# Second cross attention: the mask multiply moves from GpSimd to VectorE, both evacuations of turned probabilities to ScalarE

## The chip, the cores and the metric

The kernel runs on one core of one Trainium2 chip. The metric is the device time of one execution in microseconds (us), the median of several runs. One execution was also taken by the hardware profiler, which gives the rows below. The engines are called TensorE (PE in rows; PEld is its weight load), VectorE (DVE), ScalarE (ACT), GpSimd (POOL) and SyncE (SP, which here issues all the DMAs).

## The reference, cut to what matters

The whole program is a two-layer latent transformer: a cross attention, a linear attention and a mixture block, then a second cross attention, a multi-query attention and a second mixture. Only the second cross attention is touched. It attends from 256 query rows to 4096 key rows with 16 heads of dimension 16 and relative positions:

```python
content = einsum('bthd,bThd->bhtT', q + r_w_bias, k)
rel = einsum('bthd,bThd->bhtT', q + r_r_bias, pe)
rel = _relative_shift(rel)      # pad one column, reshape, drop one row
attn = (content + rel) * (1.0 / sqrt(HEAD_DIM))
attn = attn * mask - 1e10 * (1.0 - mask)
p = softmax(attn, axis=-1)
out = einsum('bhtT,bThd->bthd', p, v)
```

Everything is float32; the products of queries and keys are made from bfloat16 parts.

## The kernel before, in words

The function `cross1` has three blocks, and the second holds the loop. A unit of work is one head, one tile of 128 query rows and one half of the keys, so a unit is a score tile of 128x2048 and there are 16 x 2 x 2 = 64 units. Each unit is handled in two parts of 1024 columns (`SUB`). The scale is already in the queries. The tile `row` has four buffers, one for each of the four units of a head (`U = 4`).

What happens to unit c, in the order of its data:

- TensorE makes the relative scores in `rel_ps` (L1732, one PSUM tile of 128x1024), ScalarE copies them to `out0` or `out1` (L1816), and SyncE stores them to DRAM (L1683) with a row pitch of 4097, and reads them back shifted into `row` (L1672). This is done four units ahead.
- TensorE makes the content scores in `cont_ps` (L1732, also one PSUM tile of 128x1024). VectorE adds them to `row` (L1872, `add`), once for each part.
- GpSimd multiplies `row` by the mask (L1851), once for each part.
- VectorE adds `minus`, which is 1e10 * (mask - 1), and takes the maximum (L1881, `top_of`), once for each part; then small instructions make the negated maximum (L1887) and keep it (L1890).
- ScalarE takes the exponential of the whole 128x2048 tile (L1821).
- TensorE transposes the probabilities in `turn_ps` (L1750, `turn`, one PSUM tile for both parts in turn). ScalarE evacuates part 0 (L1827) and VectorE part 1 (L1897) into `turned`.
- TensorE weighs the values (L1763, `weigh`) into `sum_ps`. VectorE copies `sum_ps` to `sumsT` (L1903, `sums_out`). TensorE brings the four partial sums together in `both` (L1773, `bring_together`), and VectorE keeps the result (L1908, `keep_sums`).

All engines run the same loop of slots. In slot c each engine does, in its own written order, what its list says for units c (scores), c-1 (exponential), c-2 (turn and weigh), c-3 (sums) and c+4 (relative scores). There is no planner: the order on an engine is the program's order, and semaphores tie the engines together. TensorE's order in a slot, which the change does not touch, is: content(c, 0); bring_together(c-3), which waits for `sums_sb`, that is for VectorE's `sums_out` of unit c-3; turn(c-2, 0); relative(c+4, 0); content(c, 1), which waits until VectorE's add of part 0 has emptied `cont_ps`; turn(c-2, 1); weigh(c-2, 0); relative(c+4, 1); weigh(c-2, 1).

VectorE's order in a slot before is: top_of(c-1, 0); sums_out(c-3); add(c, 0); top_of(c-1, 1); add(c, 1); copy_turned(c-2); keep_sums(c-3).

Of the kernel before, what the change touches and what calls it, by code (L numbers as in the profile page):

```python
# [17 lines left out]
ALU = mybir.AluOpType  # L18
# [11 lines left out]
HALF = S2 // NHALF  # L30
# [1476 lines left out]
SUB = HALF // 2  # L1507
CPS = SUB // P
UNITS = H * U
# [3 lines left out]
def cross1(f, mask):  # L1513
# [8 lines left out]
    with ExitStack() as ctx:  # L1522
# [90 lines left out]
        with ExitStack() as inner:  # L1613
# [23 lines left out]
            def where(p, c):  # L1637

                return 2 * U * p + c, 2 * p + c // U, c % U, c // U % 2, c % U // NHALF, c % NHALF

            def slots(eng, slot, before=None):

                for n in range(-U, 3):
                    slot(0, n, n)
                with eng.Fori(0, LOOPS) as p:
                    for c in range(3, 3 + 2 * U):
                        slot(p, c, None)
                for n in range(2 * U * LOOPS + 3, UNITS + 3):
                    slot(LOOPS, n - 2 * U * LOOPS, n)

            def runs(n, ahead):

                return n is None or 0 <= n + ahead < UNITS
# [148 lines left out]
            @block.scalar  # L1802
            def _(act):
                act.sem_inc(s["rel_out"], 1)

                def evacuate(p, c, part):
                    n, head, u, b, t, half = where(p, c)
                    act.wait_ge(s["rel_mm"], 2 * n + part + 1)
                    if part == 0 and u >= NHALF:
                        act.wait_ge(rel_stored[u - NHALF], 16 * (head + 1))  # L1810
                    elif part == 0 and not (isinstance(n, int) and n < U):
                        act.wait_ge(rel_stored[u + NHALF], 16 * head)
                    elif part == 0 and u == 0:
                        act.wait_ge(s["zero_set"], 1)
                    out = out1 if half else out0[:, 1:HALF + 1]
                    nc.scalar.copy(out[:, part * SUB:(part + 1) * SUB], rel_ps[:]).then_inc(s["rel_out"], 1)  # L1816

                def exponentials(p, c):
                    n, head, u, b, t, half = where(p, c)
                    act.wait_ge(s["top_ready"], n + 1)  # L1820
                    nc.scalar.activation(row[:, u], row[:, u], ACT.Exp, bias=ntop[:, u:u + 1]).then_inc(s["exp_done"], 1)  # L1821

                def copy_turned(p, c):
                    n, head, u, b, t, half = where(p, c)
                    act.wait_ge(s["turned"], 2 * n + 1)
                    act.wait_ge(s["weighed"], 2 * n + 1)
                    nc.scalar.copy(turned[:, 0].rearrange("p k n -> p (k n)"), turn_ps[:]).then_inc(turned_sb[0], 1)  # L1827

                def slot(p, c, n):
                    if runs(n, -2):  # L1830
                        copy_turned(p, c - 2)
                    if runs(n, U):
                        evacuate(p, c + U, 0)
                    if runs(n, -1):
                        exponentials(p, c - 1)
                    if runs(n, U):
                        evacuate(p, c + U, 1)

                slots(act, slot)
                act.wait_ge(s["exp_done"], UNITS)  # L1840

            @block.gpsimd
            def _(pool):
                def slot(p, c, n):
                    if not runs(n, 0):
                        return
                    n, head, u, b, t, half = where(p, c)
                    for part in range(2):
                        at = part * SUB
                        pool.wait_ge(s["cont_out"], 2 * n + part + 2)  # L1850
                        nc.gpsimd.tensor_tensor(row[:, u, at:at + SUB], row[:, u, at:at + SUB],  # L1851
                                                mask[:, t, half * HALF + at:half * HALF + at + SUB],
                                                ALU.mult).then_inc(s["masked"], 1)

                slots(pool, slot)

            @block.vector
            def _(dve):
# [7 lines left out]
                def add(p, c, part):  # L1866
# [5 lines left out]
                    nc.vector.tensor_tensor(row[:, u, at:at + SUB], cont_ps[:], row[:, u, at:at + SUB],  # L1872
                                            ALU.add).then_inc(s["cont_out"], 1)

                def top_of(p, c, part):

                    n, head, u, b, t, half = where(p, c)
                    dve.wait_ge(s["masked"], 2 * n + part + 1)
                    dve.sem_inc(s["top_begun"], 1)
                    at = part * SUB  # L1880
                    nc.vector.tensor_tensor_reduce(out=row[:, u, at:at + SUB], in0=row[:, u, at:at + SUB],  # L1881
                                                   in1=minus[:, t, half * HALF + at:half * HALF + at + SUB], scale=1.0,
                                                   scalar=-3e38, op0=ALU.add, op1=ALU.max,
                                                   accum_out=top2[:, u, part:part + 1]).then_inc(s["halves_max"], 1)
                    if part == 1:
                        dve.wait_ge(s["halves_max"], 2 * n + 2)
                        nc.vector.tensor_scalar(ntop[:, u:u + 1], top2[:, u, 0:1], top2[:, u, 1:2], -1.0, ALU.max,  # L1887
                                                ALU.mult).then_inc(s["top_ready"], 1)
                        dve.wait_ge(s["top_ready"], n + 1)
                        nc.vector.tensor_copy(ntop_all[:, bass.ds(head, 1), u:u + 1], ntop[:, u:u + 1]  # L1890
                                              ).then_inc(s["top_kept"], 1)

                def copy_turned(p, c):
                    n, head, u, b, t, half = where(p, c)
                    dve.wait_ge(s["turned"], 2 * n + 2)
                    dve.wait_ge(s["weighed"], 2 * n + 2)
                    nc.vector.tensor_copy(turned[:, 1].rearrange("p k n -> p (k n)"), turn_ps[:]  # L1897
                                          ).then_inc(turned_sb[1], 1)

                def sums_out(p, c):  # L1900
                    n, head, u, b, t, half = where(p, c)
                    dve.wait_ge(s["weighed"], 2 * n + 4)
# [6 lines left out]
                                            ALU.mult).then_inc(s["sums_read"], 1)  # L1909

                def slot(p, c, n):
                    if runs(n, -1):
                        top_of(p, c - 1, 0)
                    if runs(n, -3):
                        sums_out(p, c - 3)
                    if runs(n, 0):
                        add(p, c, 0)
                    if runs(n, -1):
                        top_of(p, c - 1, 1)
                    if runs(n, 0):  # L1920
                        add(p, c, 1)
                    if runs(n, -2):
                        copy_turned(p, c - 2)
                    if runs(n, -3):
                        keep_sums(p, c - 3)

# [538 lines left out]
```

## Time and profile before

| what | value |
|---|---|
| median of 3 runs | 1565.97 us (1565.42 to 1576.41) |
| the profiled execution's own time | 1572.25 us |
| its span in the profile | 1569.4 us |
| VectorE busy over the span | 983.9 us (63%) |
| TensorE matmul busy | 1188.7 us (76%) |
| ScalarE busy | 847.4 us (54%) |
| GpSimd busy | 552.7 us (35%) |
| mean granted TensorE clock | 0.885 of full |

The profiled execution's own time is 2.85 us above its span and 6.28 us above the median. A busy share over the whole span averages stages with different limits, so the stage that is changed has to be read by itself: its loop runs from about 842 us to 1385 us of the span. "Idle before" in a row is idle time of that engine just ahead of the instruction, and what follows the arrow is what ended it.

### The profile page before, as it was taken

Reading aid. Unit: us, or ns where it says so; the run is one execution under the profiler, and the core shown is the slowest. Engines: PE = TensorE matmul, PEld = TensorE weight load, DVE = VectorE, ACT = ScalarE, POOL = GpSimd, SP = SyncE. Lnnn points to the kernel's source line nnn. Section 1 sums busy time; section 2 is a strip of 40 time slices with the busy share of each in tenths; the row PEclk is TensorE's granted clock in tenths of the full one; section 3 lists DMA queues with packets and bytes.
Section 4 is the critical chain, followed back from the end, with each engine's and each line's share of the span. In section 5 each row is a group of like instructions: output and inputs, shape, how many; then the busy total and the mean of one; then the engine's idle time right before and its main releaser. Section 6 shows DMA issues by size and latency. Waiting matters only on the chain. (4 is left out here: it accounts for less than half of the span.)

```text
span 1569.4 us, 24453 instructions
## 1 busy us (share of the span) xinstructions
PE 1188.7 (76%) x7865; PEld 716.3 (46%) x7865; DVE 983.9 (63%) x1596; ACT 847.4 (54%) x1146; POOL 552.7 (35%) x220
## 2 busy tenths in 40 slices
PE   7477777739999759979945777777777777646798
PEld 3133334323443436668831444444444444423587
DVE  5599998950111265552243999999999999834421
ACT  3499999948998124333314555555655565312210
POOL 1065666620000122000004667666776676500000
PEclk9699999969999578989975998999998999856899
DMA  7975555453443410024478999999999899333040
GB/s 268 320 249 190 182 164 190 147 165 83 109 109 81 164 68 0 1 61 154 148 227 293 326 316 318 313 307 318 312 316 315 293 308 302 106 98 111 0 153 15
DMA packets 110953, 298.23 MB, mean 190 GB/s; under 512 B 10892, under 2 KB 45618, under 8 KB 96307
## 3 DMA queue, kind: packets, MB, share of 16 engines
q1 hardware_dynamic: 110902, 297.59, 58.2%
q8 instruction: 27, 0.44, 0.1%
q14 instruction: 24, 0.20, 0.0%
HBM read 182.30 MB, written 115.25 MB: 190 GB/s over the span
## 5 line engine op out<-in xcount | busy, mean ns | idle before, releaser
L1851 POOL TENSOR_TENSOR xb_row<-xb_row,w_mask 128x1024 f32<-128x1024 f32 x128 | 360.8, 2834 | 407.4 <-DVE xb_row L1872 407.2
L1881 DVE CUSTOM_DVE_ANT_0 xb_row<-xb_row,xb_minus 128x1024 f32<-128x1024 f32 x128 | 234.2, 1830 | 0.1
L1827 ACT COPY xb_turned<-xb_turn_ps 128x1024 f32<-128x1024 f32 x64 | 64.8, 1012 | 217.6 <-PE xb_turn_ps L1750 217.6
L1872 DVE TENSOR_TENSOR xb_row<-xb_cont_ps,xb_row 128x1024 f32<-128x1024 f32 x128 | 155.7, 1216 | 41.1 <-PE xb_cont_ps L1732 32.9
L1750 PE MATMUL xb_turn_ps<-_ident,xb_row 128*128 128x128 f32 x1024 | 165.1, 314 | 16.0 <-ACT xb_turned L1827 15.2
L1750 PEld LDWEIGHTS xb_turn_ps<-_ident,xb_row 128*128 128x128 f32 x1024 | 141.5, 168 | 49.3 <-issue 47.3
L1816 ACT COPY xb_out<-xb_rel_ps 128x1024 f32<-128x1024 f32 x128 | 130.1, 1016 | 47.5 <-PE xb_rel_ps L1732 37.8
L537 DVE TENSOR_REDUCE xa_stats<-xa_b_ps 128x1 f32<-128x1024 f32 x128 | 152.9, 1217 | 4.3 <-PE xa_b_ps L436 3.9
L817 ACT ACTIVATE xa_probs<-xa_psT,xa_t_now 128x1024 f32<-128x1024 f32 x128 | 141.2, 1114 | 21.2 <-PE xa_psT L775 21.1
L486 ACT ACTIVATE xa_exps<-xa_b_ps,xa_stats 128x1024 f32<-128x1024 f32 x128 | 142.7, 1115 | 8.8 <-DVE xa_stats L537 6.5
L1821 ACT ACTIVATE xb_row<-xb_row,xb_ntop 128x2048 f32<-128x2048 f32 x64 | 128.9, 2014 | 0.4
L1732 PE MATMUL xb_rel_ps<-xb_kr,xb_qr 96*128 96x512 bf16 x256 | 91.8, 446 | 26.7 <-DMA xb_qr<-query_parts 15.0
L436 PE MATMUL xa_b_ps<-xa_k,xa_q 96*128 96x512 bf16 x256 | 77.8, 387 | 37.6 <-ACTq L475 21.2
L545 DVE CUSTOM_DVE_ANT_0 xa_squares<-xa_exps 128x1024 f32<-128x1024 f32 x64 | 87.8, 1372 | 23.7 <-ACT xa_exps L486 23.6
L1763 PE MATMUL xb_sum_ps<-xb_turned,xb_vhead 128*17 128x128 f32 x2048 | 84.9, 286 | 23.4 <-DVE xb_turned L1897 23.2
L1773 PE MATMUL xb_both<-xb_gather,xb_sumsT 128*128 128x17 f32 x128 | 25.5, 275 | 96.1 <-DVE xb_sumsT L1903 96.1
L591 POOL TENSOR_SCALAR xa_parts<-xa_whole 128x1024 bf16<-128x1024 f32 x16 | 44.3, 2770 | 150.3 <-ACT xa_whole L507 150.3
L1732 PE MATMUL xb_cont_ps<-xb_kc,xb_qc 96*128 96x512 bf16 x256 | 91.8, 446 | 2.7 <-DVE xb_row L1872 2.3
L775 PE MATMUL xa_psT<-xa_q,xa_k 99*128 (+1 forms) x512 | 79.9, 280 | 12.1 <-PE xa_sums L748 6.9
L1897 DVE COPY xb_turned<-xb_turn_ps 128x1024 f32<-128x1024 f32 x64 | 77.9, 1218 | 16.1 <-PE xb_turn_ps L1750 15.8
L457 PE MATMUL xa_b_ps<-xa_wv,xa_ctxT 128*128 x512 | 65.7, 281 | 21.1 <-ACT xa_exps L486 21.1
L748 PE MATMUL xa_sums<-xa_probs,xa_vhead 128*17 128x256 f32 x1024 | 81.0, 389 | 0.2 <-ACT xa_probs L817 0.2
(374 smaller groups left out, 1903.2 us busy)
## 6 DMA issues: line engine op xcount, KB each, us to landing
xb_row<-rel_scores SPq DMA_DIRECT2D x128, 512.0 KB, 6.2
rel_scores<-xb_out SPq DMA_DIRECT2D x32, 1024.5 KB, 6.2
rel_scores<-xb_out SPq DMA_DIRECT2D x32, 1024.0 KB, 5.0
xa_k<-key_rows SPq DMA_DIRECT2D x32, 768.0 KB, 5.4
key_rows<-xa_parts SPq DMA_DIRECT2D x24, 768.0 KB, 3.5
b_e_w<-in_L_ffn_e_w SPq DMA_DIRECT2D x32, 513.0 KB, 3.5
key_rows<-xa_parts SPq DMA_DIRECT2D x24, 512.0 KB, 4.4
xb_kr<-key_rows SPq DMA_DIRECT2D x16, 768.0 KB, 9.6
```

What stands on the lines that cost most here:

```text
L486: nc.scalar.activation(exps[:, u % 4], ps[:, slot % 4], ACT.Exp, scale=-1.0, bias=stats[:, c % 2, 0, u:u + 1], accum_out=stats[:, c % 2, 1 ...
L537: nc.vector.tensor_reduce(stats[:, c % 2, 0, u:u + 1], ps[:, slot % 4], AX, ALU.min).then_inc(s["min_ready"], 1)
L545: nc.vector.tensor_tensor_reduce(out=squares[:, 1], in0=exps[:, u % 4], in1=exps[:, u % 4], scale=1.0, scalar=0.0, op0=ALU.mult, op1=ALU.a ...
L817: nc.scalar.activation(probs[:, g % 4].rearrange("p c n -> p (c n)"), ps[:, g % 2], ACT.Exp, scale=t_now[:, b:b + 1]).then_inc(probs_ready, 1)
L1732: mm = nc.tensor.matmul(out[:, k * BANK:(k + 1) * BANK], q96[0:ROWS, bass.ds(head, 1), t * P:(t + 1) * P], k96[:, b, at:at + BANK], start= ...
L1750: mm = nc.tensor.transpose(turn_ps[:, k * P:(k + 1) * P], row[:, u, at:at + P], f.ident[:])
L1763: mm = nc.tensor.matmul(sum_ps[at:at + DV, 0:P], vhead[:, b, half * NCH // 2 + part * CPS + k, :], turned[:, part, k, :], start=(part == 0 ...
L1816: nc.scalar.copy(out[:, part * SUB:(part + 1) * SUB], rel_ps[:]).then_inc(s["rel_out"], 1)
L1821: nc.scalar.activation(row[:, u], row[:, u], ACT.Exp, bias=ntop[:, u:u + 1]).then_inc(s["exp_done"], 1)
L1851: nc.gpsimd.tensor_tensor(row[:, u, at:at + SUB], row[:, u, at:at + SUB], mask[:, t, half * HALF + at:half * HALF + at + SUB], ALU.mult).t ...
L1872: nc.vector.tensor_tensor(row[:, u, at:at + SUB], cont_ps[:], row[:, u, at:at + SUB], ALU.add).then_inc(s["cont_out"], 1)
L1881: nc.vector.tensor_tensor_reduce(out=row[:, u, at:at + SUB], in0=row[:, u, at:at + SUB], in1=minus[:, t, half * HALF + at:half * HALF + at ...
```

## The change

VectorE multiplies by the mask itself, with one instruction over the 2048 columns of a unit, which waits for the unit's two adds. GpSimd has no work in this block. ScalarE evacuates both parts of the turned probabilities; the second copy stands between evacuate(c+4, 0) and the exponential of unit c-1. VectorE's order in a slot becomes: add(c, 0); sums_out(c-3); add(c, 1); apply_mask(c); top_of(c, 0); top_of(c, 1); keep_sums(c-3). So the maximum of unit c is taken in slot c and no longer in slot c+1. TensorE's and SyncE's programs are as before.

```diff
--- before.py
+++ after.py
@@ -1820,17 +1820,20 @@
                     act.wait_ge(s["top_ready"], n + 1)
                     nc.scalar.activation(row[:, u], row[:, u], ACT.Exp, bias=ntop[:, u:u + 1]).then_inc(s["exp_done"], 1)
 
-                def copy_turned(p, c):
+                def copy_turned(p, c, part):
                     n, head, u, b, t, half = where(p, c)
-                    act.wait_ge(s["turned"], 2 * n + 1)
-                    act.wait_ge(s["weighed"], 2 * n + 1)
-                    nc.scalar.copy(turned[:, 0].rearrange("p k n -> p (k n)"), turn_ps[:]).then_inc(turned_sb[0], 1)
+                    act.wait_ge(s["turned"], 2 * n + part + 1)
+                    act.wait_ge(s["weighed"], 2 * n + part + 1)
+                    nc.scalar.copy(turned[:, part].rearrange("p k n -> p (k n)"), turn_ps[:]
+                                   ).then_inc(turned_sb[part], 1)
 
                 def slot(p, c, n):
                     if runs(n, -2):
-                        copy_turned(p, c - 2)
+                        copy_turned(p, c - 2, 0)
                     if runs(n, U):
                         evacuate(p, c + U, 0)
+                    if runs(n, -2):
+                        copy_turned(p, c - 2, 1)
                     if runs(n, -1):
                         exponentials(p, c - 1)
                     if runs(n, U):
@@ -1838,21 +1841,7 @@
 
                 slots(act, slot)
                 act.wait_ge(s["exp_done"], UNITS)
-
-            @block.gpsimd
-            def _(pool):
-                def slot(p, c, n):
-                    if not runs(n, 0):
-                        return
-                    n, head, u, b, t, half = where(p, c)
-                    for part in range(2):
-                        at = part * SUB
-                        pool.wait_ge(s["cont_out"], 2 * n + part + 2)
-                        nc.gpsimd.tensor_tensor(row[:, u, at:at + SUB], row[:, u, at:at + SUB],
-                                                mask[:, t, half * HALF + at:half * HALF + at + SUB],
-                                                ALU.mult).then_inc(s["masked"], 1)
-
-                slots(pool, slot)
+                act.wait_ge(turned_sb[1], UNITS + 1)
 
             @block.vector
             def _(dve):
@@ -1872,10 +1861,17 @@
                     nc.vector.tensor_tensor(row[:, u, at:at + SUB], cont_ps[:], row[:, u, at:at + SUB],
                                             ALU.add).then_inc(s["cont_out"], 1)
 
+                def apply_mask(p, c):
+
+                    n, head, u, b, t, half = where(p, c)
+                    dve.wait_ge(s["cont_out"], 2 * n + 3)
+                    nc.vector.tensor_tensor(row[:, u], row[:, u], mask[:, t, half * HALF:(half + 1) * HALF],
+                                            ALU.mult).then_inc(s["masked"], 1)
+
                 def top_of(p, c, part):
 
                     n, head, u, b, t, half = where(p, c)
-                    dve.wait_ge(s["masked"], 2 * n + part + 1)
+                    dve.wait_ge(s["masked"], n + 1)
                     dve.sem_inc(s["top_begun"], 1)
                     at = part * SUB
                     nc.vector.tensor_tensor_reduce(out=row[:, u, at:at + SUB], in0=row[:, u, at:at + SUB],
@@ -1890,13 +1886,6 @@
                         nc.vector.tensor_copy(ntop_all[:, bass.ds(head, 1), u:u + 1], ntop[:, u:u + 1]
                                               ).then_inc(s["top_kept"], 1)
 
-                def copy_turned(p, c):
-                    n, head, u, b, t, half = where(p, c)
-                    dve.wait_ge(s["turned"], 2 * n + 2)
-                    dve.wait_ge(s["weighed"], 2 * n + 2)
-                    nc.vector.tensor_copy(turned[:, 1].rearrange("p k n -> p (k n)"), turn_ps[:]
-                                          ).then_inc(turned_sb[1], 1)
-
                 def sums_out(p, c):
                     n, head, u, b, t, half = where(p, c)
                     dve.wait_ge(s["weighed"], 2 * n + 4)
@@ -1909,18 +1898,15 @@
                                             ALU.mult).then_inc(s["sums_read"], 1)
 
                 def slot(p, c, n):
-                    if runs(n, -1):
-                        top_of(p, c - 1, 0)
+                    if runs(n, 0):
+                        add(p, c, 0)
                     if runs(n, -3):
                         sums_out(p, c - 3)
                     if runs(n, 0):
-                        add(p, c, 0)
-                    if runs(n, -1):
-                        top_of(p, c - 1, 1)
-                    if runs(n, 0):
                         add(p, c, 1)
-                    if runs(n, -2):
-                        copy_turned(p, c - 2)
+                        apply_mask(p, c)
+                        top_of(p, c, 0)
+                        top_of(p, c, 1)
                     if runs(n, -3):
                         keep_sums(p, c - 3)
```

## Rows read from the trace of the kernel before

**Rows 1.** Windows: each engine's busy time (x instructions), granted clock, DMA share, GB/s.

```profile
866.00:1361.00 495.00, 370.33 (x3468) 221.28 (x3469) 462.44 (x664) 281.28 (x234) 337.27 (x120) 0.90 0.92 303
800.00:862.00 62.00, 27.74 (x83) 9.83 (x84) 26.43 (x44) 20.11 (x20) 15.53 (x5) 0.56 0.78 245
```

**Rows 2.** Groups of instructions, 866 to 1361 us: busy us, mean ns, idle before.

```profile
L1851 POOL TENSOR_TENSOR xb_row<-xb_row,w_mask 128x1024 f32<-128x1024 f32 x120 | 337.3, 2826 | 157.3 <-DVE xb_row L1872 157.2
...
L1821 ACT ACTIVATE xb_row<-xb_row,xb_ntop 128x2048 f32<-128x2048 f32 x60 | 120.9, 2014 | 0.3
...
L1827 ACT COPY xb_turned<-xb_turn_ps 128x1024 f32<-128x1024 f32 x60 | 60.7, 1012 | 202.2 <-PE xb_turn_ps L1750 202.2
```

**Rows 3.** Timeline, one unit from 1121 us: start, duration, engine, line.

```profile
1121.23 0.28 DVE L1903 COPY xb_sumsT<-xb_sum_ps 128x128 f32<-128x128 f32 x1
1121.43 1.21 DVE L1872 TENSOR_TENSOR xb_row<-xb_cont_ps,xb_row 128x1024 f32<-128x1024 f32 x1
...
1121.80 1.07 PE L1750 MATMUL xb_turn_ps<-_ident,xb_row 128*128 128x128 f32 x8
1122.56 1.21 DVE L1881 CUSTOM_DVE_ANT_0 xb_row<-xb_row,xb_minus 128x1024 f32<-128x1024 f32 x1
...
1122.72 5.62 POOL L1851 TENSOR_TENSOR xb_row<-xb_row,w_mask 128x1024 f32<-128x1024 f32 x2 [2.50 <-DVE xb_row L1872]
...
1123.15 0.59 PE L1732 MATMUL xb_cont_ps<-xb_kc,xb_qc 96*128 96x512 bf16 x2
...
1123.81 0.21 DVE L1887 TENSOR_SCALAR xb_ntop<-xb_top 128x1 f32<-128x1 f32 x1
...
1124.17 0.15 DVE L1890 COPY xb_ntop_all<-xb_ntop 128x1 f32 x1
1124.29 1.23 DVE L1872 TENSOR_TENSOR xb_row<-xb_cont_ps,xb_row 128x1024 f32<-128x1024 f32 x1
...
1125.43 1.22 DVE L1897 COPY xb_turned<-xb_turn_ps 128x1024 f32<-128x1024 f32 x1
...
1126.56 0.17 DVE L1908 TENSOR_SCALAR xb_o_all<-xb_both 128x17 f32 x1
...
1126.65 2.77 DVE L1881 CUSTOM_DVE_ANT_0 xb_row<-xb_row,xb_minus 128x1024 f32<-128x1024 f32 x1
...
1127.39 0.60 PE L1732 MATMUL xb_cont_ps<-xb_kc,xb_qc 96*128 96x512 bf16 x2
...
1129.35 0.28 DVE L1903 COPY xb_sumsT<-xb_sum_ps 128x128 f32<-128x128 f32 x1
```

**Rows 4.** Timeline, another unit, from 955 us.

```profile
955.88 0.28 DVE L1903 COPY xb_sumsT<-xb_sum_ps 128x128 f32<-128x128 f32 x1
...
956.46 1.89 PE L1750 MATMUL xb_turn_ps<-_ident,xb_row 128*128 128x128 f32 x8
...
958.99 1.06 PE L1732 MATMUL xb_cont_ps<-xb_kc,xb_qc 96*128 96x512 bf16 x2
...
960.09 1.23 DVE L1872 TENSOR_TENSOR xb_row<-xb_cont_ps,xb_row 128x1024 f32<-128x1024 f32 x1 [1.11 <-PE xb_cont_ps L1732]
```

**Rows 5.** Waits, 866 to 1362 us: total us, times, longest us.

```profile
PE xb_both L1773 <- DVE xb_sumsT L1903: 92.8, 61, 2.0
...
DVE xb_row L1872 <- PE xb_cont_ps L1732: 14.7, 21, 1.2
```

**Rows 6.** Timeline of VectorE in the first cross attention, from 42 us.

```profile
42.48 1.23 DVE L330 TENSOR_TENSOR xa_rest<-xa_whole,xa_parts 128x1024 f32<-128x1024 f32 x1 [0.95 <-ACT xa_parts L304]
43.74 0.69 DVE L333 CAST xa_parts<-xa_rest 128x1024 bf16<-128x1024 f32 x1
```

**Rows 7.** Timeline of VectorE ahead of the second cross attention's loop.

```profile
811.59 0.69 DVE L1604 TENSOR_TENSOR xb_rest<-xb_qb,xb_parts 128x512 f32<-128x512 f32 x1
```

**Rows 8.** Timeline: the first and the last of the loop's 61 copies of sums.

```profile
866.13 0.28 DVE L1903 COPY xb_sumsT<-xb_sum_ps 128x128 f32<-128x128 f32 x1
...
1360.67 0.28 DVE L1903 COPY xb_sumsT<-xb_sum_ps 128x128 f32<-128x128 f32 x1
```

## Prediction

> **What bounds the kernel now.** I read the windows first, because the change is confined to one loop: from 866 to 1361 us VectorE is busy 462 of 495 us, the DMA engines 0.92 of the time, TensorE 370 us, ScalarE 281 us and GpSimd 337 us [rows 1]. VectorE and the transfers are both near full, so I looked at the timeline next to see which of them sets the period. In one unit VectorE's starts join end to end [rows 3]: sums copy 1121.23, first add 1121.43, second maximum 1122.56, negated maximum 1123.81, its copy 1124.17, second add 1124.29, evacuation 1125.43, keep 1126.56, first maximum 1126.65, next sums copy 1129.35. The steps are 0.20 + 1.13 + 1.25 + 0.36 + 0.12 + 1.14 + 1.13 + 0.09 + 2.70 = 8.12 us with no gap, so VectorE's chain is the bound. Over the loop, (1360.67 - 866.13) / 60 = 8.24 us is the mean period [rows 8]; the 0.12 us above 8.12 is mostly waits of the second add for content scores, 14.7 us in 21 units [rows 5].
>
> Two more things are to be seen. The first maximum takes 2.77 us, the second 1.21, on the same shape [rows 3]: the first runs beside GpSimd's multiply, which takes 2.83 us on average [rows 2]. Its last 1.21 us would begin at 1128.2, which is where GpSimd's pair of 5.62 us from 1122.72 ends. So about 1.56 us of the 2.77 is waiting for GpSimd. And TensorE, though not the bound, waits at one place in every unit: at bring_together for VectorE's sums copy, 61 times, 92.8 us in all, up to 2.0 each [rows 5]. What stands behind that wait in its program is turn(c-2, 0), relative(c+4, 0) and content(c, 1), and content(c, 1) feeds VectorE's second add.
>
> **The change, part by part.** I add up VectorE's new chain for one slot, from the first add.
>
> *Removed.* VectorE's evacuation, 1.13 us of its chain, and the 1.57 us by which the first maximum's 2.70 exceeds the second's 1.13 to 1.14 (the add before it and the second maximum are spaced 1.13 [rows 3]). That is 2.70 us.
>
> *Added.* The mask multiply over 2048 float32 columns. No row has that size. Two SBUF inputs on VectorE cost 1.23 us for 1024 columns [rows 6] and 0.69 for 512 [rows 7], so 0.54 us for 512 more, and 1.23 + 2 x 0.54 = 2.31; I take 2.30. The bounds are 2.16 (4 x 0.54, no fixed cost at all) and 2.46 (two instructions of 1.23). It can't start until the second add is done, and the first maximum not until it is done. Such a dependent pair on VectorE starts 0.03 us after the end: 42.48 + 1.23 = 43.71, and the next at 43.74 [rows 6]. The other end is 0.15, what the copy of the negated maximum waits (1123.81 + 0.21 to 1124.17 [rows 3]). I take 0.03, which is the same kind of pair. Taken with the removals, VectorE's work alone falls: 2.70 less, about 2.45 more.
>
> *Moved.* This is where I see the cost. Before, the sums copy stands ahead of the first add, and the time from its end to the second add is filled with the first add, the second maximum and two small instructions. TensorE needs that time: the copy ends at 1121.51, turn starts 1121.80, content(c, 1) starts 1123.15 and ends 1123.74, so 2.23 us, and the second add could have started some 0.04 later; it started 1124.29, covered by 0.5 us [rows 3]. After, the sums copy stands behind the first add, and the second add is the next thing in the list. Nothing is between them. So VectorE stands idle for x, the time from the end of the sums copy to the second add. At the high clock x = 2.23 + 0.04 = 2.27. Where the clock was at its low level the same burst took, from 955.88 + 0.28 = 956.16 to the second add at 960.09, 3.93 us [rows 4]. The piece of the order that used to hide it, the second maximum, now comes later in the chain and costs its full time there.
>
> The period is then: first add to end of sums copy 1.13 + 0.28 = 1.41; x; second add to mask 1.23 + 0.03 = 1.26; mask to first maximum 2.33; first to second maximum 1.13; second maximum to negated maximum 1.25; its copy 0.36; keep 0.12; next add 0.09. Behind x that is 6.54, so period = 7.95 + x.
>
> *Which x.* In the loop before, the granted clock is 0.90 [rows 1], so one fifth of the time at 1.2 GHz and the rest at 2.4. TensorE's pause before was at most the time from the end of content(c+1, 0), 1127.39 + 0.60 = 1127.99, to the end of the sums copy at 1129.63, 1.6 us there [rows 3]. After, content(c+1, 0) still ends 3.7 us behind the start of the second add (1127.99 - 1124.29), but the next sums copy ends 6.54 + 1.41 = 7.95 behind it. The pause becomes about 4.2 us in every unit, and just behind it comes the burst that VectorE waits for. The other stretch of the rows, 800 to 862 us, where TensorE waits more than it works, was granted 0.56 [rows 1], that is nearly all at 1.2 GHz. The low level follows a pause, and the burst is what follows the pause here, so I take 19 bursts in 20 as low: x = 0.95 x 3.93 + 0.05 x 2.27 = 3.85. The lower end is a clock half way between the two stretches, 0.73, with the low level spread evenly: a low share of 0.54, x = 0.54 x 3.93 + 0.46 x 2.27 = 3.17.
>
> The Trainium skill says in "TensorE: Matmul & The Clock Gate", section Part 1, that the engine's default is half rate and that only activity releases it. If that holds after every pause of this length, all bursts are low and the sum is 1793 instead of 1788. By that rule the trace agrees in kind, since the two bursts of [rows 3] and [rows 4] ran at different levels behind a pause each; that shorter pauses leave the clock at 0.90 shows that not every pause does it.
>
> *Costed at nothing.* ScalarE's second copy is 1.01 us [rows 2]; its load rises from 281.28 / 60 = 4.7 to 5.7 us of 11.8. Queued behind the copy, which waits for turn(c-2, 1), is the exponential of c-1 (2.01 us [rows 2]), which only turn(c-1, 0) needs, in the next slot's burst. Turn(c-2, 1) follows content(c, 1) and takes 1.07 to 1.89 [rows 3, 4], so it, the copy and the exponential end 1.9 + 1.0 + 2.0 = 4.9 us behind the second add at most, and the burst starts 7.95 behind it. That leaves 3 us; were they used up, what is beyond would be paid in each unit. The transfers carry 0.92 of 8.24 = 7.6 us a unit, hidden in 11.8. GpSimd's wait and its shared use go.
>
> Sum: period 7.95 + 3.85 = 11.80, less 8.24, is 3.56 us in each of 61 units with a sums copy ahead of the second add: 217 us. The three units ahead of them and the drain behind have no such copy, but their chains are longer too; between 0 and 3 x 3.56 I take 5. So 222 us: 1572.25 becomes 1794 for the profiled execution's own time, and the median 1565.97, which is 6.28 below that, becomes 1788.
>
> **The rivals.**
>
> *Not slower: content is in time.* If x were below 8.24 - 7.95 = 0.29, the new chain would be the shorter one; with x = 0 it is 7.95, and 61 x 0.29 = 18 us less, 1548; with the mask at its upper bound it stays at 1558. For it: TensorE is idle a quarter of the loop, and VectorE's work falls. In "SBUF — State Buffer", section SBUF: two separate sides, the Trainium skill says that the loser of VectorE and GpSimd blocks entirely for the other's whole instruction; [rows 3] agrees with its 1.56 us, and this is the gain that would be seen alone. Against it: `cont_ps` is one tile, so content(c, 1) can't start until the first add ends, which alone makes x 1.21 + 0.59 + 0.04 - 1.41 = 0.43, and the program's order puts it behind the sums copy. Chance 0.03.
>
> *The stall, but at the old clock.* With low bursts in one fifth as now, x = 0.8 x 2.27 + 0.2 x 3.93 = 2.60, period 10.55, 61 x 2.31 + 5 = 146: 1712. For it: the clock recovered at once in [rows 4], where the low burst is followed by quick work. Against it: the pause more than doubles. All bursts high would be x = 2.27 and 1692. Chance 0.14 for the two together.
>
> *The stall and more.* Low bursts throughout, two waits of 0.15 and a mask of 2.46 make 7.95 + 3.93 + 0.24 + 0.16 = 12.28, 61 x 4.04 + 10 = 256: 1822. Chance 0.08.
>
> **How the numbers follow.** My forecast has 0.75: 1788, and by itself 1738 (x = 3.17, 61 x 2.88 + 5 = 181, less 9 for a mask of 2.16) to 1803 (x = 3.93, mask of 2.46). The rest is 0.14, 0.08 and 0.03. The range of 8 in 10 takes the forecast's own range and the lower part of the dearer case, and ends below it: 1730 to 1815. About 1% is what a measurement of this kernel can tell from no change. Faster by over 1% (under 1550) gets 0.01, within it 0.02, slower 0.97.
>
> **What would show it.** In the profile after, the second add of each unit (the first and second alternate) sits behind 2.3 to 3.9 us of idle time that TensorE's content scores end, some 220 us in all against 14.7; TensorE still waits for the sums copy, now about 4 us at a time; the maxima (L1881 before) are all at 1.21; the mask multiply stands at about 2.3; ScalarE's two copies follow turn at once; the DMA share falls to near 0.65, and the granted clock of the loop to some 0.6 to 0.7. The forecast is wrong if the second add follows the sums copy closely (order misread), if the clock stays near 0.9 (x too large), or if some other engine's wait stands ahead of the first add.

## The result

The changed kernel takes 1826.46 us (median of 4 runs), the kernel before 1569.3 us in the same comparison; the ratio is 1.161, with a 95% interval of 1.157 to 1.165. It is 257 us slower. The forecast was 1788 us with a range of 1730 to 1815, so the sign and the place were as told and the size was 38 us short, outside the range. The profiled execution's own time is 1826.29 us with a span of 1824.2, against 1572.25 and 1569.4 before. All ratios leave out the single executions that took over 1.5% longer than the fastest of the same kernel, among them one of the four of e5, at 2590 us, of which no trace is kept.

The same windows as [rows 1], over the 60 periods of the loop, for the changed kernel (after the length: PE, PEld, DVE, ACT, POOL busy, granted clock, DMA share, GB/s):

```profile
873.00:1616.00 743.00, 462.41 (x3468) 296.21 (x3468) 468.86 (x662) 339.72 (x294) 0.00 (x0) 0.75 0.62 201
```

VectorE was the full engine before, 462 of 495 us. Now it works 469 of 743: nearly the same amount of busy time, in half as much time again. The granted clock is 0.75 where it was 0.90, the DMA share 0.62 where it was 0.92. Nothing is full, so the loss is waiting. The first and the last of the 61 sums copies answer to [rows 8]:

```profile
873.28 0.28 DVE L1892 COPY xb_sumsT<-xb_sum_ps 128x128 f32<-128x128 f32 x1
...
1615.70 0.28 DVE L1892 COPY xb_sumsT<-xb_sum_ps 128x128 f32<-128x128 f32 x1
```

(1615.70 - 873.28) / 60 = 12.37 us for a period, against 8.24. 61 x 4.13 = 252 us of the 257 are in this loop. (The expectations and the periods of the experiments below take one copy more, from the first to the 62nd, over 61; so taken, these two are 12.34 and 8.24.) Where the waiting is, the waits of the changed kernel say (total us, times, longest):

```profile
PE xb_both L1773 <- DVE xb_sumsT L1892: 276.6, 60, 5.6
...
DVE xb_row L1861 <- PE xb_cont_ps L1732: 247.0, 60, 4.3
...
DVE xb_row L1877 <- DVE xb_row L1868: 11.2, 60, 0.2
```

The second add waits 247.0 us for content scores where it waited 14.7 [rows 5], once in each unit. That is 4.12 us a period where it was 0.24, so 3.88 of the 4.13 us that each period grew. TensorE waits 276.6 us for the sums copy, 4.6 us a time, where it was 92.8 us in 61 times. Each of the two engines waits for the other in turn. One unit of the changed kernel, from the timeline (start, duration, engine, line):

```profile
1121.51 1.22 DVE L1861 TENSOR_TENSOR xb_row<-xb_cont_ps,xb_row 128x1024 f32<-128x1024 f32 x1
...
1122.66 0.28 DVE L1892 COPY xb_sumsT<-xb_sum_ps 128x128 f32<-128x128 f32 x1
...
1122.99 0.61 PE L1773 MATMUL xb_both<-xb_gather,xb_sumsT 128*128 128x17 f32 x2 [4.37 <-DVE xb_sumsT L1892]
...
1123.44 1.95 PE L1750 MATMUL xb_turn_ps<-_ident,xb_row 128*128 128x128 f32 x8
...
1126.03 0.79 PE L1732 MATMUL xb_cont_ps<-xb_kc,xb_qc 96*128 96x512 bf16 x2
...
1126.87 1.23 DVE L1861 TENSOR_TENSOR xb_row<-xb_cont_ps,xb_row 128x1024 f32<-128x1024 f32 x1 [3.93 <-PE xb_cont_ps L1732]
...
1128.12 2.29 DVE L1868 TENSOR_TENSOR xb_row<-xb_row,w_mask 128x2048 f32<-128x2048 f32 x1
...
1129.37 0.60 PE L1732 MATMUL xb_cont_ps<-xb_kc,xb_qc 96*128 96x512 bf16 x2
...
1130.60 1.23 DVE L1877 CUSTOM_DVE_ANT_0 xb_row<-xb_row,xb_minus 128x1024 f32<-128x1024 f32 x1 [0.19 <-DVE xb_row L1868]
...
1133.52 0.18 DVE L1897 TENSOR_SCALAR xb_o_all<-xb_both 128x17 f32 x1
1133.75 1.23 DVE L1861 TENSOR_TENSOR xb_row<-xb_cont_ps,xb_row 128x1024 f32<-128x1024 f32 x1
1134.89 0.28 DVE L1892 COPY xb_sumsT<-xb_sum_ps 128x128 f32<-128x128 f32 x1
...
1139.37 1.23 DVE L1861 TENSOR_TENSOR xb_row<-xb_cont_ps,xb_row 128x1024 f32<-128x1024 f32 x1 [4.20 <-PE xb_cont_ps L1732]
```

In each unit there are two stretches in which one of the two engines stands still. From 1122.94, the end of the sums copy, to 1126.87 VectorE does nothing and TensorE does bring_together, turn, relative and content. From 1129.97 to 1134.89 + 0.28 = 1135.17 TensorE has nothing it may do, and VectorE does the rest of the mask multiply, the maxima and the next first add. The last row is the second add of the next unit, with 4.20 us of idle time. Only in the 3.1 us between, from 1126.87 to 1129.97, do both work.

The groups of instructions show that the other parts did what they were to do:

```profile
L1877 DVE CUSTOM_DVE_ANT_0 xb_row<-xb_row,xb_minus 128x1024 f32<-128x1024 f32 x120 | 142.3, 1223 | 11.2 <-DVE xb_row L1868 11.2
L1868 DVE TENSOR_TENSOR xb_row<-xb_row,w_mask 128x2048 f32<-128x2048 f32 x60 | 137.5, 2292 | 2.1
```

All maxima take 1.22 us, none is blocked, and the mask multiply over 2048 columns takes 2.29.

### The profile page after: what moved, and what is told of

It is laid out like the page before. It is cut to its first block and busy times, and to the rows that moved or that the text cites. A ratio compares the mean times of both kernels' runs of the same rounds, so it can differ in the third digit from the quotient of the medians.

```text
span 1824.2 us, 24407 instructions
## 1 busy us (share of the span) xinstructions
PE 1290.6 (71%) x7865; PEld 798.0 (44%) x7865; DVE 993.2 (54%) x1596; ACT 909.7 (50%) x1210; POOL 191.8 (11%) x92
## 5 line engine op out<-in xcount | busy, mean ns | idle before, releaser
L1827 ACT COPY xb_turned<-xb_turn_ps 128x1024 f32<-128x1024 f32 x128 | 129.6, 1012 | 424.9 <-PE xb_turn_ps L1750 424.9
L1773 PE MATMUL xb_both<-xb_gather,xb_sumsT 128*128 128x17 f32 x128 | 37.2, 371 | 284.1 <-DVE xb_sumsT L1892 284.1
L1750 PE MATMUL xb_turn_ps<-_ident,xb_row 128*128 128x128 f32 x1024 | 226.9, 396 | 3.7 <-ACT xb_turned L1827 3.7
L1750 PEld LDWEIGHTS xb_turn_ps<-_ident,xb_row 128*128 128x128 f32 x1024 | 204.2, 222 | 38.2 <-issue 37.2
L1773 PEld LDWEIGHTS xb_both<-xb_gather,xb_sumsT 128*128 128x128 f32 x128 | 30.3, 294 | 315.6 <-DVE xb_sumsT L1892 283.6
L1877 DVE CUSTOM_DVE_ANT_0 xb_row<-xb_row,xb_minus 128x1024 f32<-128x1024 f32 x128 | 151.8, 1223 | 11.9 <-DVE xb_row L1868 11.9
L1868 DVE TENSOR_TENSOR xb_row<-xb_row,w_mask 128x2048 f32<-128x2048 f32 x64 | 146.7, 2292 | 2.2
L1732 PE MATMUL xb_rel_ps<-xb_kr,xb_qr 96*128 96x512 bf16 x256 | 109.5, 521 | 24.3 <-DMA xb_qr<-query_parts 14.9
L1732 PE MATMUL xb_cont_ps<-xb_kc,xb_qc 96*128 96x512 bf16 x256 | 107.0, 511 | 8.6 <-DVE xb_row L1861 8.2
L457 PEld LDWEIGHTS xa_b_ps<-xa_wv,xa_ctxT 128*128 128x128 f32 x512 | 59.6, 191 | 36.7 <-ACT xa_exps L486 31.3
```

The lines of the kernel that those rows point to most:

```text
L457: mm = nc.tensor.matmul(out[:, n * P:(n + 1) * P], ctxT[:, k, at:at + P], wv[:, bass.ds(it, 1), k, :], start=(k == 0), stop=(k == KC - 1))
L1732: mm = nc.tensor.matmul(out[:, k * BANK:(k + 1) * BANK], q96[0:ROWS, bass.ds(head, 1), t * P:(t + 1) * P], k96[:, b, at:at + BANK], start= ...
L1750: mm = nc.tensor.transpose(turn_ps[:, k * P:(k + 1) * P], row[:, u, at:at + P], f.ident[:])
L1827: nc.scalar.copy(turned[:, part].rearrange("p k n -> p (k n)"), turn_ps[:]).then_inc(turned_sb[part], 1)
L1868: nc.vector.tensor_tensor(row[:, u], row[:, u], mask[:, t, half * HALF:(half + 1) * HALF], ALU.mult).then_inc(s["masked"], 1)
```

## The experiments

Ratios are to the kernel before, run on the same chip beside each kernel, with 95% intervals. The burst is TensorE's run of bring_together, turn, relative and content, from the end of the sums copy to the second add. The order theory is that the new order on VectorE (the sums copy behind the first add, the second maximum no longer between the adds) leaves nothing to cover this burst. The rivals were VectorE's added work, and for single points those named in each expectation.

**e1, the sums copy first.**

```diff
 def slot(p, c, n):          # VectorE, changed kernel
+    if runs(n, -3):
+        sums_out(p, c - 3)
     if runs(n, 0):
         add(p, c, 0)
-    if runs(n, -3):
-        sums_out(p, c - 3)
```

> The changed kernel with the sums copy ahead of the first add. Order theory: the burst on TensorE from the sums copy to the second add keeps its 4.06 us, but the first add (1.15 us) now runs under it, so the period falls from 12.34 to about 11.2 us and the time by 61 x 1.14 = 70 us to about 1756. Rival, that VectorE's added work and its dependent waits make the loss: nothing of either is changed, about 1826.

Measured: 1719.55 us, ratio 1.094 (1.089 to 1.098). One call moved by one place gives back 107 us. Added work alone is refuted, since none was taken away. But it is 37 us more than I expected. The window and TensorE's wait for the sums copy (869 to 1500 us) say why:

```profile
900.00:1439.00 539.00, 368.79 (x2958) 227.19 (x2958) 399.22 (x567) 293.17 (x255) 0.00 (x0) 0.80 0.75 242
```
```profile
PE xb_both L1773 <- DVE xb_sumsT L1892: 197.2, 61, 4.1
```

The clock is 0.80 where the changed kernel has 0.75, and the pause is 3.2 us on average where it was 4.6. The length of bring_together's two matmuls shows at which level a burst begins: 0.40 us at the high one, 0.61 at the low. In the 61 units of the loop 53 bursts begin low in the changed kernel, 20 in e1 and 1 in the kernel before, whose pauses are 1.5 us on average. Bursts of e1 that begin high can still fall within, as in this one, where turn runs at the high level and content at the low:

```profile
1125.62 0.29 DVE L1892 COPY xb_sumsT<-xb_sum_ps 128x128 f32<-128x128 f32 x1 [0.36 <-issue]
1125.86 1.22 DVE L1861 TENSOR_TENSOR xb_row<-xb_cont_ps,xb_row 128x1024 f32<-128x1024 f32 x1
...
1126.28 1.07 PE L1750 MATMUL xb_turn_ps<-_ident,xb_row 128*128 128x128 f32 x8
...
1127.98 1.06 PE L1732 MATMUL xb_cont_ps<-xb_kc,xb_qc 96*128 96x512 bf16 x2
...
1129.08 1.22 DVE L1861 TENSOR_TENSOR xb_row<-xb_cont_ps,xb_row 128x1024 f32<-128x1024 f32 x1 [2.00 <-PE xb_cont_ps L1732]
```

From the copy's end, 1125.91, to the second add is 3.17 us, of which the first add fills 1.17. Over the loop the time from the copy's end to the second add is 3.42 us on average, against 4.11 in the changed kernel. I had held it at 4.06 and not reckoned that the move also shortens the pause ahead of the burst.

**e2, VectorE's old order around the new work.**

```diff
 def slot(p, c, n):          # VectorE, changed kernel
+    if runs(n, -1):
+        top_of(p, c - 1, 0)
+    if runs(n, -3):
+        sums_out(p, c - 3)
     if runs(n, 0):
         add(p, c, 0)
-    if runs(n, -3):
-        sums_out(p, c - 3)
+    if runs(n, -1):
+        top_of(p, c - 1, 1)
     if runs(n, 0):
         add(p, c, 1)
         apply_mask(p, c)
-        top_of(p, c, 0)
-        top_of(p, c, 1)
```

> The changed kernel with VectorE's old order around the new mask multiply: first maximum of c-1, sums copy, first add, second maximum of c-1, second add, mask multiply, keep. All of the work that the change moved stays moved. Order theory: the second maximum and its two small instructions again lie between the sums copy and the second add, the period is VectorE's work, 0.20 + 1.13 + 1.25 + 0.36 + 0.12 + 1.25 + 2.35 + 0.12 + 1.15 = 7.9 us plus what the low clock adds, 8.0 to 8.3, so 1553 to 1575. Rival, the added work: about 1800.

Measured: 1564.33 us, ratio 0.994 (0.991 to 0.996). All of the work stays where the change put it and all of the 257 us are gone. Of these, e1 had given back 107; the other 155 or so come with the second maximum and its small instructions, which stand ahead of the second add again; a little of it is that the mask multiply no longer stands right ahead of the maximum that needs it. This is the run that decides: the mask on VectorE and both evacuations on ScalarE cost nothing, the order costs everything. One of its units:

```profile
1121.68 0.28 DVE L1892 COPY xb_sumsT<-xb_sum_ps 128x128 f32<-128x128 f32 x1
1121.88 1.21 DVE L1861 TENSOR_TENSOR xb_row<-xb_cont_ps,xb_row 128x1024 f32<-128x1024 f32 x1
...
1123.01 1.21 DVE L1877 CUSTOM_DVE_ANT_0 xb_row<-xb_row,xb_minus 128x1024 f32<-128x1024 f32 x1
...
1123.60 0.59 PE L1732 MATMUL xb_cont_ps<-xb_kc,xb_qc 96*128 96x512 bf16 x2
...
1124.27 0.21 DVE L1883 TENSOR_SCALAR xb_ntop<-xb_top 128x1 f32<-128x1 f32 x1
...
1124.75 1.22 DVE L1861 TENSOR_TENSOR xb_row<-xb_cont_ps,xb_row 128x1024 f32<-128x1024 f32 x1
...
1126.01 2.29 DVE L1868 TENSOR_TENSOR xb_row<-xb_row,w_mask 128x2048 f32<-128x2048 f32 x1
```

Content ends at 1124.19 and the second add starts at 1124.75: the second maximum and its small instructions cover it again.

**e3, TensorE's order instead.**

```diff
 # TensorE, changed kernel, between content(p, c, 0) and turn(p, c - 2, 1)
-    if runs(n, -3):
-        bring_together(p, c - 3)
     if runs(n, -2):
         turn(p, c - 2, 0)
     if runs(n, U):
         relative(p, c + U, 0)
     if runs(n, 0):
         content(p, c, 1)
+    if runs(n, -3):
+        bring_together(p, c - 3)
```

> The changed kernel, VectorE's new order kept, but TensorE brings the sums together behind content(c, 1), so that content(c, 1) no longer stands behind the wait for the sums copy. Order theory: the second add then waits only for the one cont_ps tile, 0.4 to 1.0 us behind the sums copy; the period is 8.28 + 0.4 to 1.0, the time 1826 - 61 x (4.06 - 0.4 to 1.0) = 1603 to 1640. Rival, that cont_ps itself or the added work is what holds the second add: above 1780.

Measured: 1615.39 us, ratio 1.023 (1.018 to 1.029). This takes the same wait away from the other side, and VectorE keeps the changed order:

```profile
1121.54 1.23 DVE L1861 TENSOR_TENSOR xb_row<-xb_cont_ps,xb_row 128x1024 f32<-128x1024 f32 x1
...
1122.68 0.28 DVE L1892 COPY xb_sumsT<-xb_sum_ps 128x128 f32<-128x128 f32 x1
...
1122.82 0.60 PE L1732 MATMUL xb_cont_ps<-xb_kc,xb_qc 96*128 96x512 bf16 x2 [1.50 <-DVE xb_row L1861]
...
1123.46 1.22 DVE L1861 TENSOR_TENSOR xb_row<-xb_cont_ps,xb_row 128x1024 f32<-128x1024 f32 x1 [0.51 <-PE xb_cont_ps L1732]
```

Turn and relative have run ahead, content starts 0.05 us behind the first add, and the second add waits 0.50 us behind the sums copy's end, for the one tile of content scores. The prediction had bounded this at 0.43. Over the loop the second add waits 37.3 us in 60 times, 0.62 each, where it was 4.12. So what held the second add was that content stood behind bring_together's wait; the single tile is worth about half a microsecond. The rest of the chain is as in the changed kernel, and e3 stays 2.3% behind the kernel before.

**e5, TensorE kept busy in the pause.** The 14 matmuls multiply the identity by itself into `turn_ps`, which the next turn overwrites; they first wait until `turn_ps` has been evacuated.

```diff
     if runs(n, -3):
+        pe.wait_ge(turned_sb[1], where(p, c - 2)[0] + 1)
+        for _ in range(14):
+            nc.tensor.matmul(turn_ps[:, 0:P], f.ident[:], f.ident[:], start=True, stop=True)
         bring_together(p, c - 3)
```

> The changed kernel with 14 more matmuls (identity by identity, into turn_ps, overwritten by the turn that follows) in TensorE's pause ahead of its wait for the sums copy. They only keep TensorE busy. Clock theory: the burst behind the pause runs at 2.4 GHz, x falls from 4.06 to about 2.3 us, and the time by 61 x 1.76 = 107 us to about 1719; a half of the bursts would give 1773. Rival, that the clock has no part in it: 1826, or more where the extra matmuls run into the burst.

Measured: 1724.04 us, ratio 1.095 (1.090 to 1.101). More work on TensorE, 102 us less time, and 5 us above what I expected if the clock has its part. The window, the second add's waits from 872 to 1510 us, and one unit:

```profile
900.00:1447.00 547.00, 450.31 (x4410) 339.23 (x4409) 401.04 (x566) 294.46 (x257) 0.00 (x0) 0.98 0.75 239
```
```profile
DVE xb_row L1864 <- PE xb_cont_ps L1732: 141.5, 60, 4.0
```
```profile
1123.56 3.29 PE L1785 MATMUL xb_turn_ps<-_ident 128*128 128x128 f32 x28
...
1128.42 0.28 DVE L1895 COPY xb_sumsT<-xb_sum_ps 128x128 f32<-128x128 f32 x1
...
1129.07 1.07 PE L1750 MATMUL xb_turn_ps<-_ident,xb_row 128*128 128x128 f32 x8
...
1130.41 0.59 PE L1732 MATMUL xb_cont_ps<-xb_kc,xb_qc 96*128 96x512 bf16 x2
...
1131.05 1.22 DVE L1864 TENSOR_TENSOR xb_row<-xb_cont_ps,xb_row 128x1024 f32<-128x1024 f32 x1 [2.34 <-PE xb_cont_ps L1732]
```

The clock is 0.98, and from the end of the sums copy, 1128.70, to the second add is 2.35 us where the changed kernel has 3.93 in the unit shown. The second add's wait is 141.5 / 60 = 2.36 us on average. So of its 4.12 us in the changed kernel, about 2.4 are the order and 1.8 the low level of the burst behind the pause. It is the order that made the pause, so the two are one loss. The Trainium skill says in "TensorE: Matmul & The Clock Gate", section Part 1, that half rate is the engine's default and that activity releases it. This run agrees: with the pause filled, the clock is 0.98.

**e4, the evacuation alone, from the kernel before.**

```diff
 # ScalarE, kernel before: a second copy as in the changed kernel
+    if runs(n, -2):
+        copy_turned(p, c - 2, 1)     # behind evacuate(p, c + U, 0)
 # VectorE, kernel before
-    if runs(n, -2):
-        copy_turned(p, c - 2)
```

> The kernel before with one part of the change alone: ScalarE evacuates both parts of the turned probabilities; GpSimd still multiplies by the mask and VectorE keeps its old order, less the evacuation. Shadow theory: VectorE's evacuation (1.13 us of its chain) ran while the first maximum would have waited for GpSimd anyway, and GpSimd's two multiplies and the two maxima exclude each other (2 x 2.36 + 2 x 1.21 = 7.1 us, plus the waits between them) while the transfers take 7.6 us a unit: period 7.6 to 8.1, ratio to the kernel before 0.975 to 1.00. Rival, the plain sum: 1.13 us off each period, 61 x 1.13 = 69 us, ratio 0.956.

Measured: 1590.04 us, ratio 1.013 (1.009 to 1.017). Both expectations missed, the plain sum by 5.7% and the shadow theory by a little: an instruction less on the full engine makes the kernel slower. The period is 8.55 us, where it was 8.24:

```profile
1120.01 1.21 DVE L1885 CUSTOM_DVE_ANT_0 xb_row<-xb_row,xb_minus 128x1024 f32<-128x1024 f32 x1
...
1120.09 5.67 POOL L1855 TENSOR_TENSOR xb_row<-xb_row,w_mask 128x1024 f32<-128x1024 f32 x2 [2.91 <-DVE xb_row L1876]
...
1121.35 1.21 DVE L1876 TENSOR_TENSOR xb_row<-xb_cont_ps,xb_row 128x1024 f32<-128x1024 f32 x1
...
1123.63 3.21 DVE L1885 CUSTOM_DVE_ANT_0 xb_row<-xb_row,xb_minus 128x1024 f32<-128x1024 f32 x1 [1.07 <-POOL xb_row L1855]
...
1128.66 3.36 POOL L1855 TENSOR_TENSOR xb_row<-xb_row,w_mask 128x1024 f32<-128x1024 f32 x1 [2.91 <-DVE xb_row L1876]
```

VectorE comes to the first maximum sooner, 0.08 us before GpSimd begins the unit's second multiply, and it is not blocked, 1.21 us. But that multiply, beginning behind it, takes long (3.36 us in the next unit, the last row, where the shortest take 2.34) and is not done when the second maximum needs it: the wait of 1.07 us ahead of 1123.63. And in the meantime GpSimd has started the next unit's first multiply, which blocks the second maximum to 3.21 us; its last 1.21 begin at 1125.63, near the end of GpSimd's pair at 1125.76. So 3.07 us of waiting stand where 1.13 of evacuation and 1.56 of blocking stood. That the order of the two starts decides who blocks whom is read from these rows; no run shifts one engine against the other by itself.

**e6, no mask multiply.** It leaves the multiplication by the mask out of e2, and the maximum waits for the unit's adds instead.

```diff
         add(p, c, 1)
-        apply_mask(p, c)
...
 # top_of
-    dve.wait_ge(s["masked"], n + 1)
+    dve.wait_ge(s["cont_out"], 2 * n + part + 2)
```

> VectorE's old order with both evacuations on ScalarE, as in e2, and the multiplication by the mask left out altogether (the maximum and minus stay). VectorE's chain is then about 8.16 - 2.45 = 5.7 us. If VectorE's work were the only bound: 61 x 2.4 = 149 us less than e2, ratio to the kernel before about 0.90. Transfer theory: the transfers need 0.92 x 8.24 = 7.6 us a unit, so the period stops there, ratio about 0.97.

Measured: 1534.36 us, ratio 0.976 (0.971 to 0.981). The waits (900 to 1268 us) name the next bound, and the window shows how full it is:

```profile
DVE xb_row L1861 <- DMA xb_row<-rel_scores: 103.5, 82, 2.8
```
```profile
900.00:1268.00 368.00, 286.66 (x2772) 166.54 (x2772) 256.11 (x478) 273.55 (x238) 0.00 (x0) 0.93 0.98 330
```

The adds wait for the rows read back from DRAM, and the DMA share is 0.98. With 2.3 us a unit less on VectorE only 0.018 of the ratio, 28 us, came off e2. The transfers allow this loop no less than about 7.65 us a unit.

**e7, e8 and e10, bring_together moved in the better kernels.** e7 is e2 with e3's edit, e8 is the kernel before with e3's edit alone, and e10 is e7 once more.

> e2 with TensorE's bring_together behind content(c, 1) as well. The second add then never waits for the sums copy. e2 lost about 8.16 - 7.96 = 0.2 us a unit to bursts at the low clock; without them 61 x 0.2 = 12 us less, ratio to the kernel before about 0.986. Rival, that the pauses only move to another place on TensorE: ratio 0.994 as e2.

> The kernel before with nothing changed but TensorE's bring_together behind content(c, 1). It takes away the 14.7 us for which the second add waited for content scores; the chain of 8.12 us stays. Ratio about 0.991 to 0.996. Rival, that the first maximum's wait for GpSimd takes up what the second add gains (both multiplies follow the adds): 1.00.

> e7 once more, beside e9 on the same chip. Ratio to the kernel before 0.982 to 0.989, as e7 gave, whatever theory holds; e9's gain is read against this.

Measured: e7 1547.48 us, ratio 0.986 (0.982 to 0.989), and again as e10 1549.72, 0.985 (0.982 to 0.989). e8 1561.18 us, ratio 0.993 (0.990 to 0.995). In e7, from 900 to 1273 us, the second add waits for content once:

```profile
DVE xb_row L1861 <- PE xb_cont_ps L1732: 0.2, 1, 0.2
```

e7 is faster than both kernels, by 1.4% than the kernel before. Between e8 and e7, both free of this stall, stand the moves of work alone: periods 8.11 and 7.96 us, worth 61 x 0.15 = 9 us by the periods and 0.7% by the ratios.

**e9, the copy that keeps the negated maximum on GpSimd.** From e7:

```diff
 # VectorE, end of top_of
-    dve.wait_ge(s["top_ready"], n + 1)
-    nc.vector.tensor_copy(ntop_all[:, bass.ds(head, 1), u:u + 1], ntop[:, u:u + 1]).then_inc(s["top_kept"], 1)
 # GpSimd, one for each unit
+    pool.wait_ge(s["top_ready"], n + 1)
+    nc.gpsimd.tensor_copy(ntop_all[:, bass.ds(head, 1), u:u + 1], ntop[:, u:u + 1]).then_inc(s["top_kept"], 1)
... (and VectorE waits for top_kept before it makes the next negated maximum)
```

> e7 (mask on VectorE, both old orders of dependence restored) with the one-column copy that keeps the negated maximum on the idle GpSimd. It takes 0.35 + 0.12 us of VectorE's chain less what the next instruction still waits, about 0.33 us of 7.96, so 7.6; the transfers' 7.65 of e6 is then the bound: period 7.65 to 7.7, ratio to the kernel before 0.973 to 0.977. Rival, that GpSimd's small copy blocks VectorE's two-input instructions or that the transfers are already the bound in e7 (share 0.97): 0.986 as e7.

Measured: 1545.27 us, ratio 0.984 (0.979 to 0.988), beside 0.985 for e10 on the same chip. The expected 0.973 to 0.977 lies below the interval, 0.979 to 0.988, so that is missed; and the intervals of e9 and e10 overlap, so whether it gains at all is open as a time. In the traces the period is 7.77 against e10's 7.96. The negated maximum is at 1119.41 and the second add now at 1119.54, where e2 had 0.48 us between them, and the DMA share is 0.98, up from 0.97:

```profile
1119.41 0.21 DVE L1897 TENSOR_SCALAR xb_ntop<-xb_top 128x1 f32<-128x1 f32 x1
1119.54 1.21 DVE L1874 TENSOR_TENSOR xb_row<-xb_cont_ps,xb_row 128x1024 f32<-128x1024 f32 x1
```

The chain of VectorE is shorter, as meant. That the transfers took up the rest of the gain is not shown; their share of 0.98 fits it.

## Why the prediction was right in its place and wrong in its size

The mechanism was as told. The steps that failed are two terms of the sum, x (the time from the sums copy's end to the second add) and the gaps in the rest of VectorE's chain: I had 3.85 + 7.95 us, and the runs show 4.12 + 8.25.

*What bounds the kernel.* Right for the work in its new places: e2 and e7 show VectorE's chain as the period (8.16 and 7.96 us), and e6 the transfers behind it at 7.65; I had worked out 7.6. For the kernel before it was told too simply. Its chain of 8.12 holds 1.56 us of waiting for GpSimd, and e4 shows that 1.13 us less work on VectorE does not shorten the loop, because the waiting grows. Nor is the 0.12 us between 8.12 and 8.24 mostly the second add's waits. These are 14.7 / 60 = 0.24 a period, and the unit of [rows 3] has a first maximum of 2.77 where the average of the loop is about 2.49 (both maxima together 3.70, one 1.21):

```profile
L1881 DVE CUSTOM_DVE_ANT_0 xb_row<-xb_row,xb_minus 128x1024 f32<-128x1024 f32 x121 | 224.1, 1852 | 0.0
```

The sum does not hang on either, since it adds up the new chain by itself and takes the measured 8.24 from it.

*Removed and added.* The relief of the first maximum came as told (1.22 us after). The mask multiply is 2.29 us where I took 2.30. I had 2.70 off and about 2.45 on, 0.25 us less; with the old order on VectorE and bring_together moved in both, e7 against e8 measured 0.15.

*Moved.* Right, and the core of it. The wait, its place, its releaser and the engine that waits for the other are as told. e1, e2 and e3 each undo it from another side. e2 and e3 came in the ranges that its length gave; e1 gave back 107 us where I had expected 70, for the reason told there.

*Which x.* Here the first part of the error lies. I took 3.85, a near-certain low level on the length of the burst of [rows 4], 3.93. The wait of the second add is 4.12 on average. Nearly every burst is low, as I had said (53 of 61 from their start), but the burst of [rows 4] was not low from its start: its turn began 956.46 - 956.16 = 0.30 us behind the sums copy, as quickly as at the high level, while in the changed kernel the turn begins 1123.44 - 1122.94 = 0.50 behind it, and bring_together takes 0.61. Bursts that are low throughout took 4.20 (the row at 1139.37). I called a burst fully low whose first two matmuls were not. 0.27 us in each of 61 periods are 16 us. The granted clock of the loop, foretold at some 0.6 to 0.7, is 0.75 all the same: what TensorE does behind the burst runs high again, such as content in 0.60 at 1129.37.

*The dependent pairs.* The second part. I took 0.03 us behind the end of the instruction waited for and named 0.15 as the other end. The second add to the mask multiply was indeed 0.02 (1128.10 to 1128.12), but the mask multiply to the first maximum 0.19 (1130.41 to 1130.60), in all 60 (11.2 us of waits). From the start of keep to the next add it is 0.20 on average, where I took 0.09: 0.14 in most units, 0.23 in some (1133.52 to 1133.75) and about 0.7 in five, ahead of whose adds VectorE waits for nothing that the profile shows. What makes these gaps is open. The copy of the negated maximum to keep is 0.15 instead of 0.12. All that is not x came to 12.37 - 4.12 = 8.25 instead of 7.95: 61 x 0.30 = 18 us. Both parts together are 34 us. By the profiled execution's own time the forecast was 1794 and the measured 1826.29, 32 short, and these two parts are that. The median was 38 short because I took 6.28 off for the distance of the profiled execution from it, and in the changed kernel that distance is nothing (1826.29 against 1826.46).

*The range.* Both misses were terms with named other ends, and they go the same way. I priced them together at 1822, gave that 0.08, and let the range stop under it at 1815. Both upper ends, 3.93 and 0.15, were themselves taken from too mild a place.

*Costed at nothing.* ScalarE's second copy cost nothing (e2), as told. But I never asked what that one move does by itself: e4 shows that taking the evacuation off VectorE costs 1.3% while GpSimd still multiplies by the mask.

*The rivals.* Not slower: e2, e7 and e9 are where that case would be, and it needs the order kept. The stall at the old clock: e5, whose bursts are nearly all high, took 1724 where I had priced 1692; 18 of the 32 us between are the 0.30 us of the dependent pairs, which e5 has too.

## What to carry to other kernels

When instructions are reordered on one engine, look on the other engine for what stands in program order behind each wait on it. Here a copy of 0.28 us moved behind an add of 1.2 us, and the second maximum no longer stood ahead of the next add. That cost 4 us a unit, because bring_together and three groups of matmuls stood behind the copy's semaphore and the next add needed the last of them. Moving the copy alone back gives 107 us of it (e1), the second maximum with it all (e2). Such a wait is bought off on either side: fill the time on the one engine (e2), or move the waiting instruction behind those that others need (e3); here both are best (e7). And where a change makes a long pause on TensorE, give the work behind it a dear case at 1.2 GHz from its first matmul. With pauses of 4.6 us on average this was the rule (53 of 61), with 3.2 us one burst in three (20 of 61), with 1.5 us one in 61.

## What the runs showed that I had not expected

- The low level after a pause is a large part of such a loss (1.8 of 4.1 us) and can be bought off with useless work: 14 extra matmuls in each pause (e5) brought the clock from 0.75 to 0.98 and took 102 us off.
- VectorE's start behind its own result is not one number: 0.02 to 0.03 us from a 1024-column add to the mask multiply, 0.19 from the 2048-column multiply to the maximum, in every unit.
- VectorE's maximum and GpSimd's multiply block each other, and by the rows of e4 the one that starts second is the one that waits: taking 1.13 us off VectorE made the loop 0.3 us a unit slower (e4).
